# A two-layer adaLN transformer with top-2 experts on one core: router logits with the gate stationary, a gate folded into the last experts, modulation issued earlier, some score products issued twice, new order tables

## The reference, cut to what matters

```python
x = L0_attn_x                                             # (8, 512, 128)
# layer 0, then layer 1; mod = (silu(c) @ wmod) -> sa, ca, ga, sb, cb, gb
h = layernorm(x) * (1 + ca) + sa
x = x + ga * attn(h)            # 16 heads of 8; layer 0 full, layer 1 causal and with latent projections
h = layernorm(x) * (1 + cb) + sb
x = x + gb * ffn(h)
# ffn: scores = softmax(h @ gate); the top 2 of 8 experts, weighted by their scores
# layer 0: silu(h @ w1) * (h @ w3) @ w2 per expert, plus a shared expert of the same kind
# layer 1: relu(h @ W1)^2 @ W2 per expert
```

## Time and profile before

| | us |
|---|---|
| median of three executions | 1061.68 (1061.51 to 1062.42) |
| the profiled execution, its own time | 1055.22 |
| its span, first to last instruction | 1053.5 |
| PE, DVE, ACT, POOL busy in it | 976.7, 824.4, 743.0, 454.5 |

### The profile page before, as it was taken

The page is one execution under the profiler, slowest core; times in us unless marked ns, Lnnn a source line. Parts: engine busy times, 40 slices in busy tenths (PEclk is TensorE's granted clock), DMA queues, the critical chain, the costliest instruction groups (busy, mean ns, idle before and its releaser), DMA issues.

```text
span 1053.5 us, 27436 instructions
## 1 busy us (share of the span) xinstructions
PE 976.7 (93%) x10743; PEld 529.7 (50%) x10743; DVE 824.4 (78%) x1672; ACT 743.0 (71%) x1225; POOL 454.5 (43%) x545
## 2 busy tenths in 40 slices
PE   7678898879999999999999999999999999999997
PEld 5211222222645455345655666666765555455565
DVE  6888899787999888678977688777877567677456
ACT  4347876668575766987577775666866988877864
POOL 5130121144024435641344742456644566836553
PEclk9858998899999999999999999999999989999999
DMA  6832525254664686584765896777887857411000
GB/s 186 209 115 53 144 73 147 77 168 128 186 204 121 216 247 178 157 246 147 244 203 165 259 278 196 223 208 227 262 260 227 234 167 183 111 62 56 33 12 21
DMA packets 120480, 174.73 MB, mean 166 GB/s; under 512 B 19896, under 2 KB 84280, under 8 KB 120352
## 3 DMA queue, kind: packets, MB, share of 16 engines
q1 hardware_dynamic: 114096, 159.87, 51.3%
q0 software_dynamic: 5680, 12.33, 4.0%
q10 hardware_dynamic: 576, 0.79, 0.3%
HBM read 114.21 MB, written 58.59 MB: 164 GB/s over the span
## 4 chain that ended last, share of the span: by engine, by line
PE 58%; DVE 20%; DMA 7%; ACT 6%; issue 5%; POOL 3%; SPq 1%; POOLq 0%; DVEq 0%; ACTq 0%
PE ps L748 19%; PE ps L873 13%; DVE nm L1082 12%; PE ps L750 8%; PE ps L856 7%; PE ps L834 6%; ACT ES L1429 3%; DMA gr<-d_y,pos 2%; DMA d_h<-hx,pos 1%; ACT xn L1354 1%; DMA d_h<-r,pos 1%; PE ps L776 1%; PE ps L905 1%; PE ps L839 1%; DMA DR<-d_r 1%
## 5 line engine op out<-in xcount | busy, mean ns | idle before, releaser
L1082 DVE TENSOR_REDUCE nm<-ps 128x2 f32<-128x1024 f32 (+3 forms) x512 | 504.6, 1019 | 106.9 <-PE ps L839 63.0
L1429 ACT ACTIVATE ES<-ps 128x1024 f32<-128x1024 f32 (+1 forms) x448 | 418.1, 961 | 104.4 <-PE ps L856 67.2
L873 PE MATMUL ps<-ES,VS 128*9 128x512 f32 (+3 forms) x2048 | 223.2, 522 | 0.4 <-DVE r L1268 0.2
L834 PE MATMUL ps<-KS,QS 48*128 48x512 bf16 (+3 forms) x1024 | 173.4, 354 | 31.0 <-DVE nm L1082 19.5
L856 PE MATMUL ps<-QS,KS 51*128 51x512 bf16 (+3 forms) x1024 | 168.6, 348 | 12.7 <-DVE nm L1082 6.4
L834 PEld LDWEIGHTS ps<-KS,QS 48*128 48x128 bf16 x1024 | 49.1, 94 | 145.9 <-DVE nm L1082 51.1
L856 PEld LDWEIGHTS ps<-QS,KS 51*128 51x128 bf16 x1024 | 50.2, 94 | 137.1 <-ACT ES L1429 44.7
L748 PE MATMUL ps<-hsT,wst 128*128 128x128 f32 x784 | 111.1, 285 | 2.8 <-DVE r L1275 1.6
L1657 POOL DMA_INDIRECT gr<-d_y,pos x80 | 83.3, 1041 | 64.2 <-DMA gr<-d_y,pos 35.7
L748 PEld LDWEIGHTS ps<-hsT,wst 128*128 128x128 f32 x784 | 95.2, 191 | 21.2 <-issue 17.4
L1583 POOL TENSOR_TENSOR sp<-sr,sp 128x512 bf16<-128x512 f32 x32 | 37.2, 1171 | 85.2 <-ACT sp L1390 85.1
(11 more groups left out here) (229 smaller groups left out, 1541.8 us busy)
## 6 DMA issues: line engine op xcount, KB each, us to landing
wst<-we SPq DMA_DIRECT2D x92, 576.0 KB
d_u<-US SPq DMA_DIRECT2D x60, 256.0 KB
KS<-d_k SPq DMA_DIRECT2D x62, 192.0 KB, 4.8
QS<-d_q SPq DMA_DIRECT2D x62, 192.0 KB, 5.4
hs<-d_h SPq DMA_DIRECT2D x25, 256.0 KB
d_y<-ys SPq DMA_DIRECT2D x25, 256.0 KB, 5.6
d_q<-sp SPq DMA_DIRECT2D x16, 384.0 KB, 3.0
d_k<-sp SPq DMA_DIRECT2D x16, 384.0 KB, 3.7
```

Of the source, the lines that this page charges most:

```text
L834: mm = eng.matmul(psum[:, bank[u][a], c:c + n], QS[m][r:r + KA, pr, 128 * t1:128 * t1 + 128], KS[m][r:r + KA, pr, 0:n], start=True, stop=i ...
L873: mm = eng.matmul(psum[32 * a:32 * a + 9, b, q0:S], VS[i % 3][:, j1, 4 * g + a, :], ES[(2 * EXP[i, g, j] + a // 2) % NES][:, a % 2, c:c + ...
L1082: ins = eng.tensor_reduce(nm[f][:, :].rearrange("p (a c) -> p a c", a=2)[:, :, 4 * pr + t1], ps2("score", i, f, pr, t)[:, :, c:c + n], AX. ...
L1429: eng.activation(ES[(2 * n + pp) % NES][:, :, 0:w], ps2("bscore", i, f, g, j, pp)[:, :, 0:w], ACT.Exp, scale=SC1 if i >= NB else SC0).then ...
```

## The change

Five things:

1. `f_gate` takes the gate's 8 columns as the stationary operand and the 128 tokens of a tile as the moving one; the four tiles write to partitions 0, 32, 64 and 96 of one bank, so in the four column strips of the array. ACT copies the 128x128 result to a new buffer `gT` (`f_gt`), PE transposes it (`f_back`), and `f_lg` reads the logits from PSUM, without the copy. So 16 DVE copies go, 16 ACT copies and 16 PE transposes come.
2. For sequence 15 POOL multiplies the eight experts' second weights by gb once (`d_rg`, into `rg`), `d_y` adds each expert straight to `X`, `d_xv` is gone, and the result leaves in two halves of 128 KB, the first after half of the last `d_y` (`d_end`).
3. Layer 1's `m_s2`, `m_mm` and `m_gm` come ahead of `p_turn` of sequence 1, with six identity products between.
4. `MORE_S` and `MORE_B` name 40 `score` and 24 `bscore` pieces of sequences 0 to 7 whose products are issued once more (three of them twice more) into the same place: 67 more pairs. All but three of these pieces belong to sequences 0 to 5.
5. New numbers in the four tables, so a new order on all engines.

```diff
-SHIFT = {"bscore": -0.04, "c": -0.94, "d": 15.58, "early": -20.01,
+SHIFT = {"bscore": -0.04, "c": -16.7, "d": 26.54, "early": -28.49,
...
+MORE_S = {
+    (0, 0, 0, 3): 1, (0, 0, 2, 2): 1, (0, 0, 3, 0): 1, (0, 0, 3, 2): 1, (0, 1, 1, 1): 1, (0, 1, 1, 2): 1,
...
-        add("PE", ("m_mm", l), 1.5 if l else 2.8, u, [("m_s2", l), ("m_ld", l)] + ([("p_v", 0)] if l else [("c_warm", 0)]), opens=1)
+        add("PE", ("m_mm", l), 2.8, u, [("m_s2", l), ("m_ld", l)] + ([("m_gm", 0)] if l else [("c_warm", 0)]), opens=1, closes=[("c_warm", 0)] if l else [])
...
-        add("PE", ("f_gate", i), 0.81, u, [("f_ht", i)], opens=1)
-        add("DVE", ("f_lg", i), 0.58, u, [("f_gate", i), ("f_idx", i - 1)], closes=[("f_gate", i)])
+        add("PE", ("f_gate", i), 0.24, u, [("f_ht", i)], mode="cols", opens=1)
+        add("ACT", ("f_gt", i), 0.19, u, [("f_gate", i), ("f_back", i - 1)], closes=[("f_gate", i)])
+        add("PE", ("f_back", i), 0.11, u, [("f_gt", i)], opens=1)
+        add("DVE", ("f_lg", i), 0.4, u, [("f_back", i), ("f_idx", i - 1)], closes=[("f_back", i)])
...
+                add("POOL", ("d_rg",), 2.6, u - 1.0, [("t_gt", i), ("ld", "r2"), ("x_dn",) + UNITS[-1]])
...
-                        mm = eng.matmul(ps(*u)[:, E * t:E * t + E], hFs[i][:, 128 * t:128 * t + 128],
-                                        ws[:, W["g"]:W["g"] + E], start=True, stop=True)
+                        mm = eng.matmul(ps(*u)[32 * t:32 * t + E, 0:128], ws[:, W["g"]:W["g"] + E],
+                                        hFs[i][:, 128 * t:128 * t + 128], start=True, stop=True, skip_group_check=True)
...
+                elif k == "f_back":
+                    q.wait_ge(*on("f_gt", u[1]))
+                    open_banks(u)
+                    eng.transpose(ps(*u)[:, 0:128], gT[:, :], ident[:, :]).then_inc(s[k], 1)
...
+                        for t in range(NT):
+                            xs = X[:, NT * (i % NB) + t, :]
+                            ins = eng.scalar_tensor_tensor(out=xs, in0=yv[:, t, :], scalar=combs[i][:, t, e:e + 1], in1=xs,
+                                                           op0=ALU.mult, op1=ALU.add)
+                            if k == "d_end" and t % 2:
+                                ins.then_inc(s["d_end"], 1)
```

More of the change, by code:

```diff
@@ new lines @@
+LATE = {"bscore": 0.01, "c": 19.16, "d": -2.55, "early": -13.05, "expo": 23.45, "f": -2.64, "g": 7.82, "ld": 18.63, "m": -11.22, "max": -30.65, "p": -16.16, "r": 27.31, "rowmax": 7.18, "rr": -14.21, "s": 25.03, "score": 0.02, "stack": -53.64, "t": -3.93, "u": -28.23, "v": 10.39, "w": -54.04, "x": 5.06}
+LAST = {"bscore": 0.07, "c": 18.27, "d": -7.64, "early": -3.01, "expo": -15.13, "f": -10.37, "g": 2.34, "ld": -4.67, "m": 28.49, "max": -29.21, "p": -8.83, "pv": 39.32, "r": -3.13, "rowmax": 66.96, "rr": 5.35, "s": -45.61, "score": 0.14, "stack": -0.08, "t": 10.96, "u": 19.3, "v": 22.08, "w": -40.88, "x": 7.71}
@@ L518, in plan @@
                 else:
-                    add("PE", ("d_dn", i, e), 0.89, u, [(sq, i, e), ("d_comb", i), ("d_y", i, e - 2)], mode="any", opens=1)
+                    add("PE", ("d_dn", i, e), 0.89, u, [(sq, i, e), ("d_comb", i), ("d_y", i, e - 2), ("d_rg",)], mode="any", opens=1)
                 if i == N - 1:
-                    add("DVE", ("d_y", i, e), 0.8 if e else 0.61, u, [("d_dn", i, e), ("d_comb", i), ("d_y", i, e - 1)] + [("r_sc", len(GROUPS) - 1, t, c) for t in range(GROUPS[-1][1] * NT - 2, GROUPS[-1][1] * NT) for c in range(2)], closes=[("d_dn", i, e)])
+                    add("DVE", ("d_y", i, e) if e < E - 1 else ("d_end", i), 1.1, u, [("d_dn", i, e), ("d_comb", i), ("t_add", i), ("d_y", i, e - 1)],
+                        closes=[("d_dn", i, e)])
                 elif e == 0:
@@ L528, in plan @@
             if i == N - 1:
-                add("DVE", ("d_xv", i), 1.2, u, [("d_y", i, E - 1), ("t_gt", i), ("t_add", i)])
-                add("SP", ("d_out", i), 0.5, u, [("d_xv", i)])
+                for h in range(2):
+                    add("SP", ("d_out", i, h), 0.45, u, [("d_end", i)])
             else:
@@ L1293, in _ @@
                     q.wait_ge(*on("d_comb", i))
[L1294 to L1303 removed]
+                    if i == N - 1:
+                        q.wait_ge(*(on("d_y", i, e - 1) if e else on("t_add", i)))
+                        for t in range(NT):
+                            xs = X[:, NT * (i % NB) + t, :]
[3 more added lines that the diff above has]
+                                ins.then_inc(s["d_end"], 1)
+                        if k == "d_y":
+                            ins.then_inc(s["d_y"], 1)
                     elif e == 0:
@@ L1442, in _ @@
                     eng.activation(OT[:, :], ps("v_back"), ACT.Copy).then_inc(s[k], 1)
+                elif k == "f_gt":
+                    i = u[1]
+                    if i:
+                        q.wait_ge(*on("f_back", i - 1))
+                    q.wait_ge(*on("f_gate", i))
+                    eng.activation(gT[:, :], ps("f_gate", i)[:, 0:128], ACT.Copy).then_inc(s[k], 1)
                 elif k == "f_exp":
@@ L1862, in _ @@
             q.wait_ge(s["ld", "out"], 16 * (NB - 1))
-            q.wait_ge(s["ld", "last"], 16)
+            q.wait_ge(s["ld", "last"], 32)
 def kernel(**inputs):
```

115 lines of the change are left out of this document (52 added, 63 removed), and 28 rows, old and new, of tables (MORE_B, MORE_S, NUDGE).

## The result

| | before | changed |
|---|---|---|
| median of 20 executions on one chip | 1063.35 (1058.31 to 1068.22) | 1057.60 (1049.52 to 1068.39) |
| ratio, with its 95% interval | | 0.9944 (0.9923 to 0.9965) |
| the profiled execution, its own time | 1055.22 | 1053.87 |
| its span | 1053.5 | 1051.9 |
| mean granted clock in it | 0.967 | 0.983 |

The change is faster, by 0.56% or about 6 us; forecast were 11 us, 1.04%.

What follows compares the result with a forecast made beforehand. PE was taken to bound the kernel from 300 to 1008 us, DVE to be tighter before 300. Terms -3.5 - 5 - 1.5 + 2 - 3 = -11.0 gave a median of 1050.7 us, range 1042 to 1061.

Steps and rivals of the forecast that it cites:

- early modulation: At the start, layer 1's modulation ahead of sequence 1's transposes: earlier first maximum, no m_fin between maxima; -3.5 us.
- router: Router product in column strips: 0.50 us less PE work per sequence, 6.5 us over 13, less 1.5 of stalls; -5 us.
- gate folded, the end: At the end, the store waits on the last sum alone and its second half is 128 KB; -1.5 us.
- repeats, less the clock they win: Before 300 us, 67 repeated score pairs cost +2 us and the clock they buy gives -3.
- new order: New order on all engines: no row tells its worth; taken as 0, with 6 us either way for the range.
- Rival (e): New waits of the new order, 11 us or so, use up the gain: near 1062 us; chance 0.08.
- 21.9:28.7: Stretch at the start, in us, where early modulation and six identity products keep PE working, so the clock doesn't fall.
- Rival (c): PE stalls at f_back for ACT's copy, up to 1.3 us a router, deciding from 0.6: 1073 us; chance 0.06.
- Both stretches that I named: 69.7:76.5 and 199.4:206.2 us, at 1.2 GHz before: full clock there worth 1.9 and 3.4 us.
- the two terms, +2 and -3: Repeated scores: +2 us for their PE work (bounds 0 and +14.7), -3 for the clock won (bounds 0 and -5.3).
- 55.0:69.7: Stretch in us at 1.2 GHz where DVE works without a gap and PE is partly idle: low clock costs nothing.
- The frame of the sum: Sum made against the profiled execution's 1055.22 us, carried to the median 1061.68, assuming their 6.5 us difference does not change.

Runs made afterwards that it cites:

- e15: Changed kernel's order and early modulation alone, with the old router, old end and no repeated scores: 1065.40 us, 1.0034 of the kernel before.
- e18: Kernel before in its own order, with layer 1's modulation and six identity products early and m_fin ahead of the maxima: 1059.00 us, 0.9952 of before.
- e16: Changed kernel with layer 1's modulation put back in its old place, without its identity products: 1062.27 us, 0.9983 of the kernel before.
- set 3: Four variants of the changed kernel on a slower chip, where the kernel before takes 1074.16 us: 1.0133, 1.0053, 1.0021 and 1.0129 of before.
- e7: Changed kernel in its own order with the old router product, without ACT's copy and the transpose: 1060.31 us, 1.0012 of the kernel before.
- e2: Changed kernel without the 67 repeated score pairs, same order on every engine: 1057.40 us, 0.9944 of the kernel before.
- e14: Changed kernel in its own order without repeated scores and with the old end: 1058.21 us, 0.9962 of the kernel before.
- e1: The changed kernel, measured once more: 1054.39 us, 0.9923 of the kernel before.
- e6: Kernel before in its own order, with the gate folded into the last sequence's experts alone: 1060.88 us, 1.0004 of before.

## Why the prediction was half right

| term | forecast | alone, old order | in the changed kernel |
|---|---|---|---|
| early modulation | -3.5 | -5.1 | -6.3 |
| router | -5 | -3.9 | -7.6 |
| gate folded, the end | -1.5 | +0.4 (-2.0 at the end itself) | } |
| repeats, less the clock they win | -1 | +8.1 | } -4.0 together |
| new order | 0 | | +8.7 (e15 less e18), +9.9 (e15 less e16's step) |
| whole | -11 | | -6 to -8 |

**The step that failed is "The new order ... I take 0".** I said that no row tells what it is worth, which was true, and then put it at the value in the middle. It costs some 9 us. That the gain is still over half of my 11 is partly luck: within the new order the other terms add up to 18 us where I had 11, and those 7 us cover most of the order's cost. Of the four, only the repeats are clearly worth more in the new order than in the old (some 2 to 3 us of gain for 8.1 of loss); for router and modulation the intervals overlap. My ground for the zero was off too: the two PE lists have half of their pieces within 3 places of each other, but the farthest is 80 away, and not some thirty. Rival (e), new waits of the new order that use up the gain, had 0.08 of the chance. It named the right part and, at 11 us, nearly its size, but the parts gained more than it was to use up, so it did not come out as (e) priced it, 1062. On the slow chip of set 3 it may well describe the whole.

**The modulation** was right in place, its size within the intervals: first maximum at 27.8 forecast, 27.1 to 27.7 found where the clock stayed up, 28.9 in the profiled execution where it fell at 23.8. My claim that the clock then stays up in 21.9:28.7 holds in half of the cases: of the 12 profiles with the early modulation six read 1.00 there and six 0.75, and all six fixed-order profiles without it read 0.50. Whether the identity products do that, or the place alone, was not tried apart.

**The router**: 0.50 us less on PE was forecast, 0.56 found where it was read; behind 300 us the new router takes some 4 us off PE's busy time (e7 against the changed kernel), forecast 6.5. The stalls were undersized, 6.0 us of waits for `gT` for my 1.5. Yet the part measured 3.9 and 7.6 us for my 5, so some of the waits cost nothing. Rival (c) needed 0.6 us a router; the nine waits are 0.67 each, but seven of the 16 have none, and that brings the mean to 0.38.

**Repeats and clock.** Both stretches that I named went in the profiled execution, one of them by luck: 199.4:206.2 is at full clock in e2 without repeats, and in e14, e15 and e18 too. Wrong was that the two terms, +2 and -3, are a property of the repeats. The same 67 pairs are worth 8 us of loss in one order and, by e1 against e2, 2 to 3 of gain in the other, within an interval of some 3 us either way. I had seen that the low clock costs nothing in 55.0:69.7, because DVE was without a gap there, and did not ask what 20 doubled pairs of sequence 0 do to PE in just that stretch: it filled, and DVE is busy 11.66 to 12.63 of 14.70 (13.46 in the new order without repeats, 14.70 before).

**The end** came as written, 2.0 us for 1.5, with the first store out before the last sum is done. e6's median can't tell whether the two products on POOL take some of it back.

**The frame of the sum** failed as well. I carried the sum from the profiled execution to the median and assumed that the 6.5 us between them stay. For the changed kernel they are 3.7 (1057.60 less 1053.87), and 8.1 for before by the median of 20. The profiled execution of before is an unusually short one.

## What to carry to other kernels

Where a planner or tables set the order, measure a part with the order held fixed: put through the planner again, two parts that in the fixed order gave 0.996 and 1.000 cost 4% and 1%. A new order is not a zero term: here it cost some 9 us by itself. Products that are issued again to hold the clock up must be tried in the very order in which they will run; the same 67 pairs gave 2 to 3 us in one and took 8 in the other. And a gain of 0.7% in a kernel this tight should be measured on more than one chip: on one of those used here it was likely gone.
